# A chunked linear-attention block in fp32: correction products from two inverses, key work moved to GpSimd, keys kept unexpanded

## Chip, cores and metric

The kernel runs on one core of one Trainium2 chip. The metric is the device time of one execution in microseconds (us). Engines are named as in the profile: PE is TensorE (PEld its weight loads), DVE is VectorE, ACT is ScalarE, POOL is GpSimd, SP is SyncE.

## What is computed

Input is one sequence of 4096 tokens of width 256, all in fp32. A layer norm with modulation is followed by an attention without a softmax over tokens, and then by a mixture of experts. Cut to what matters:

```python
q, k, v = x @ Wq, x @ Wk, x @ Wv              # 8 heads of 64
beta, tg = sigmoid(x @ Wbeta), sigmoid(x @ Wtg)   # 8 modes a head
qr = l2norm(rotary(q, cos, sin)) * scale      # angles = pos * omega[h, m] * inv_freq
kr = l2norm(rotary(k, cos, sin))
g  = log(clip(tg * rho, 1e-6))
def step(S, inp):                             # one token; 64 memories (head, mode) of 64x64
    S  = S * exp(g_t)
    kv = k_t . S
    dv = (v_t - kv) * beta_t
    S  = S + k_t (x) dv
    o_t = q_t . S
x = x + ga * ((sum over modes of mode_w * o) * sigmoid(x @ Wg)) @ Wo
# then: layer norm, router, top 2 of 8 experts, capacity 1024, gelu, weighted sum
```

## The kernel before

**Tiles, halves, chunks.** The recurrence is worked in chunks of 32 tokens. A tile is 128 tokens (4 chunks), and there are 32 tiles. A tile is done in two halves (hh = 0 and 1), each of 4 heads; the 64 modes and heads are held as 16 groups ("quads") of 4 modes, 8 to a half. Partitions carry mode (4) x frequency or token (32). `u = 2n + hh` counts halves. The loop body of each engine is `half(n, 1)` followed by `half(n + 1, 0)`, so the jump back to the loop's start falls between an hh = 0 half and the hh = 1 half behind it.

**What a half does.** It prepares its own keys, queries and decays, builds the triangular systems of its 4 chunks, and inverts them on DVE (`solve`, L1226: 31 steps of two passes, then a transpose that writes `tt` and raises `tt_ready`, L1240). In the meantime the four chunks of the half before (called v) go through the chain of the memories, chunk after chunk:

- PE `memory_read` (L535): keys times state, into `bank_mem`; keys come from `ke`, which is expanded so that a key of 32 rows stands in a 128-row block with zeroes.
- DVE `right_sides` (L1242): times the decay `eg_col`, and the values minus that, into `rhs`.
- PE `corrections` (L553): the inverse `tt` times `rhs`, in 32x32 tiles of the array (L563), and then the state times the queries (L569).
- ACT `take_dv` (L760): fades the state (L765) and copies the corrections to `dv` (L769). DVE `decayed_corrections` (L1258) scales them to `dvs`.
- PE `update_and_outputs` (L573): expanded turned keys `kte` times `dvs` (L582), and the outputs (L590).
- DVE `update_memories` (L1266): adds the update to the state and takes the outputs.

Then the next chunk's `memory_read` may start.

**Where the keys come from.** PE replicates keys and queries (`replicate`, L485). DVE rotates keys (`rotate_keys`, L1175: four products and two sums), POOL rotates queries from ACT's copy `raw` (L1485 to L1490, `q_rotated`). ACT expands the rotated keys (`expand_ke`, L796, 4 passes a chunk) and the keys that DVE turned (`turn_keys`, L1202; `expand_kte`, L752, 4 passes a chunk). PE `gram` (L497) makes the products of keys with keys and queries for a chunk, and DVE `chunk_systems` (L1219) takes them. DVE also works out the six passes of `angle_parts` (L1112) for the next half; PE `turn_sums` (L624) uses them.

**What sets the order.** Every engine runs its own `half` in the order that is written there; a wait holds up all that is behind it. On PE (L644) the replications and the decay rows stand between the chunks of the chain, `gram(u, 0)` behind the corrections of chunk 3, and the other three behind its update. On ACT (L816) sine and cosine stand between chunks 0 and 1, the copies `raw` and the exponentials of the decays between chunks 1 and 2. On DVE (L1332) the chain's passes are woven between its own work.

## Time and profile before

| | |
|---|---|
| runs of the kernel before | 7991.04, 8003.09, 8010.95 us (median 8003.09) |
| the profiled execution | 7953.85 us, span 7951.7 us |
| mean granted TensorE clock | 0.82 of full speed |
| PE busy, x instructions | 5413.0 us (68%), 111401 |
| DVE busy, x instructions | 5656.2 us (71%), 11457 |
| ACT busy, x instructions | 3642.4 us (46%), 7127 |
| POOL busy, x instructions | 1241.2 us (16%), 740 |
| HBM traffic | 11 GB/s over the span |

Busy time is an average over three stages: a set-up of some 200 us, the loop over tiles up to about 7330 us, and the experts with their combination behind that. The change touches only the first two. One fp32 matmul of the source is two MATMUL instructions in the profile, each with its LDWEIGHTS. In the timeline a row is a run of like instructions on one engine: start, length, engine, line, operation, tiles and shapes, their count, and in brackets the idle time before it and what ended that.

### The profile page before, as it was taken

The page shows a single profiled execution, that of the slowest core. Times are in us where ns is not written, and L with a number is a line of the kernel's source. Part 1 is how long each engine was busy: PE and PEld are TensorE (multiplying, and loading weights), DVE is VectorE, ACT ScalarE, POOL GpSimd, SP SyncE. Part 2 cuts the span into 40 slices and gives each one's busy share as a digit, 9 for nine tenths or more (in the row PEclk, how much of TensorE's full clock was granted, in tenths as well). Part 3 has the DMA queues.
Part 4 walks back from the last instruction along what each step waited for, and adds up shares of the span by engine and source line. Part 5 has one row for each costly group of instructions (what it writes and reads, how often), then busy time and mean ns, then how long its engine had stood idle before and what let it go on. Part 6 is the DMA issues. An engine that isn't in the chain of part 4 may idle for free. (4 is left out here: it accounts for less than half of the span.)

```text
span 7951.7 us, 264166 instructions
## 1 busy us (share of the span) xinstructions
PE 5413.0 (68%) x111401; PEld 4716.2 (59%) x111401; DVE 5656.2 (71%) x11457; ACT 3642.4 (46%) x7127; POOL 1241.2 (16%) x740
## 2 busy tenths in 40 slices
PE   0676667666776677666766667666676667766994
PEld 0666656556666666566665666556666556655663
DVE  6777777777777777777777787777777777776003
ACT  0454445544544455544544455544454445554220
POOL 0111111111111111111111111111111111111003
PEclk9787888777877787887878888888887888887997
DMA  2000000000000000000000000000000000000223
GB/s 75 2 6 6 6 6 4 4 6 6 6 6 6 6 4 6 4 6 6 6 6 6 6 4 6 4 6 6 6 6 6 6 6 4 6 4 9 87 75 95
DMA packets 60431, 104.35 MB, mean 13 GB/s; under 512 B 11296, under 2 KB 48736, under 8 KB 58080
## 3 DMA queue, kind: packets, MB, share of 16 engines
q1 hardware_dynamic: 50784, 61.66, 2.4%
q0 software_dynamic: 8448, 25.18, 1.0%
q8 instruction: 940, 15.40, 0.8%
q14 instruction: 259, 2.12, 0.1%
HBM read 53.25 MB, written 33.55 MB: 11 GB/s over the span
## 5 line engine op out<-in xcount | busy, mean ns | idle before, releaser
L765 ACT ACTIVATE state<-state,gc_end 128x128 f32<-128x128 f32 x2048 | 650.1, 389 | 1432.4 <-PE bank L569 1430.9
L563 PE MATMUL bank<-rhs,tt 32*32 32x64 f32 x16384 | 407.0, 248 | 874.7 <-DVE rhs L1256 874.6
L563 PEld LDWEIGHTS bank<-rhs,tt 32*32 32x32 f32 x16384 | 316.3, 125 | 961.5 <-issue 944.4
L582 PE MATMUL last_two<-dvs,kte 128*64 128x64 f32 x16384 | 716.4, 254 | 150.3 <-DVE dvs L1263 150.3
L634 PE MATMUL bank<-tmp,turn_mat 32*32 32x128 f32 x24576 | 745.3, 279 | 48.4 <-issue 34.1
L545 PE MATMUL bank<-state,ke 128*64 128x64 f32 x16384 | 647.3, 246 | 167.3 <-issue 128.8
L582 PEld LDWEIGHTS last_two<-dvs,kte 128*64 128x64 f32 x16384 | 655.1, 167 | 164.9 <-DVE dvs L1263 157.2
L634 PEld LDWEIGHTS bank<-tmp,turn_mat 32*32 32x32 f32 x24576 | 709.8, 110 | 71.5 <-issue 65.4
L800 ACT ACTIVATE ke<-kq 32x512 f32<-32x512 f32 x1024 | 641.9, 627 | 238.1 <-DVE kq L1191 226.0
L545 PEld LDWEIGHTS bank<-state,ke 128*64 128x64 f32 x16384 | 605.2, 159 | 238.9 <-issue 184.2
L1239 DVE TENSOR_TENSOR last_two<-last_two,prod 128x31 f32<-128x31 f32 (+15 forms) x1984 | 692.5, 349 | 68.1
L506 PE MATMUL bank<-kq,ke 128*64 128x64 f32 x16384 | 638.6, 250 | 124.1 <-DVE pw L1224 115.6
L1237 DVE TENSOR_TENSOR prod<-bd,last_two 128x31 f32<-128x31 f32 (+15 forms) x1984 | 671.1, 338 | 68.3
L756 ACT ACTIVATE kte<-kt 32x512 f32<-32x512 f32 x1024 | 641.4, 626 | 142.9 <-PE last_two L582 125.0
L506 PEld LDWEIGHTS bank<-kq,ke 128*64 128x64 f32 x16384 | 617.8, 165 | 129.8 <-DVE pw L1224 77.6
L1272 DVE TENSOR_TENSOR state<-last_two,state 128x512 f32<-128x512 f32 x512 | 354.1, 692 | 205.1 <-PE last_two L582 172.9
L1263 DVE TENSOR_TENSOR dvs<-bank,dec_end 128x256 f32<-128x256 f32 x512 | 217.3, 424 | 363.3 <-PE bank L569 354.6
L1485 POOL TENSOR_TENSOR tmp<-raw,cos_t 128x1024 f32<-128x1024 f32 x64 | 151.2, 2362 | 2007.8 <-ACTq L839 2007.8
L480 PE MATMUL bank<-row_group,select 128*128 128x128 f32 x3072 | 434.4, 298 | 6.9 <-DVE tmp L1187 5.6
L569 PE MATMUL bank<-qg,state 128*64 128x32 f32 x8192 | 410.5, 250 | 0.3 <-issue 0.3
L480 PEld LDWEIGHTS bank<-row_group,select 128*128 128x128 f32 x3072 | 395.4, 207 | 24.7 <-DVE tmp L1187 6.4
L1461 POOL DMA_INDIRECT expert_rows<-xn,scatter_at x64 | 64.0, 999 | 2166.1 <-DVE scatter_at L1325 2156.3
(236 smaller groups left out, 9821.8 us busy)
## 6 DMA issues: line engine op xcount, KB each, us to landing
w_sb<-in_L_ffn_W_dram SPq DMA_DIRECT2D x16, 1024.0 KB, 9.6
expert_rows<-ke SPq DMA_DIRECT2D x1, 8192.0 KB, 21.0
xrows<-expert_rows SPq DMA_DIRECT2D x16, 512.0 KB, 8.7
expert_outputs<-yrow POOLq DMA_DIRECT2D x16, 512.0 KB, 3.4
xt<-_attn_hidden_states_dram SPq DMA_DIRECT2D x32, 128.0 KB, 2.4
xr<-_attn_hidden_states_dram SPq DMA_DIRECT2D x32, 128.0 KB, 3.0
x_after_attention<-xr SPq DMA_DIRECT2D x32, 128.0 KB, 1.7
xo<-x_after_attention SPq DMA_DIRECT2D x32, 128.0 KB, 3.6
```

What stands on the lines that cost most here:

```text
L480: mm = pe.matmul(b[:, ql * P:ql * P + P], select[:, b4 * 4 + ql, :], row_group[:, group, :], start=True, stop=True)
L506: mm = pe.matmul(b[s, q * 2 * C:(q + 1) * 2 * C], ke[:, c, r, q, s], kq[:, r, q, :, c * C:c * C + C], start=(r == 0), stop=(r == 1))
L545: mm = pe.matmul(bank_mem[g][s, q % 4 * DK:q % 4 * DK + DK], ke[:, c, r, q, s], state[:, hh * HQ + q, r, :], start=(r == 0), stop=(r == 1))
L563: pe.matmul(bank_mem[g][s, q % 4 * DK:q % 4 * DK + DK], tt[s, c, q, :], rhs[s, q, :], start=True, stop=True)
L569: mm = pe.matmul(out_bank(g, side), state[:, hh * HQ + q, r, :], qg[:, r, q, c * C:c * C + C], start=(j == 0 and r == 0), stop=False)
L582: mm = pe.matmul(bank_upd[g][s, (q % 4) * P + r * DK:(q % 4) * P + r * DK + DK], kte[:, r, q, s], dvs[:, q, :], start=True, stop=True)
L634: mm = pe.matmul(b[s, ql * P:ql * P + P], turn_mat[s, 2 * i + kind, hh * HQ + q, :], tmp[s, part, q * P:q * P + P], start=(i == 0), stop=( ...
L756: ins = act.activation(kte[s, :, :, 32 * m:32 * m + 32].rearrange("p r q f -> p (r q) f"), kt[s, :, :, c * C:c * C + C].rearrange("p r q f ...
L765: ins = act.activation(state[:, vh * HQ + q], state[:, vh * HQ + q], ACT.Copy, scale=gc_end[:, vh, q, c:c + 1])
L800: ins = act.activation(ke[s, c, :, :, 32 * m:32 * m + 32].rearrange("p r q j -> p (r q) j"), kq[s, :, :, 0, c * C:c * C + C].rearrange("p ...
L1237: ln(dve.tensor_tensor(pr, a_prob[:, j + 1:C, j:j + 1].broadcast_to([P, rows, cols]), t_prob[:, j:j + 1, 0:cols].broadcast_to([P, rows, co ...
L1239: ln(dve.tensor_tensor(below, below, pr, ALU.subtract))
```

## The change

The chain's corrections become two products a chunk: `tt` times the values, plus `tt_eg` (the inverse times the decay, made by POOL) times the negated read `ks`, which ACT copies. DVE's `right_sides` and `decayed_corrections` are gone. The update uses `dv` itself; the decay to the chunk's end is put on the turned keys by POOL (`fade_keys`, in place). The expanded `ke` and `kte` are gone: reads, updates and `gram` use 32x32 tiles over four modes where they used two sides of 64 columns. POOL adds the products of the key rotation, and takes over `angle_parts`. DVE's order changes with it.

```diff
 def gram(u, hh, c):
     pe.wait_ge(sem("q_rotated"), since("q_rotated", u + 1))
-    pe.wait_ge(sem("ke_ready"), 4 * u + c + 1)
+    pe.wait_ge(sem("k_rotated"), since("k_rotated", u + 1))
...
-                for s in SIDES:
-                    mm = pe.matmul(b[s, q * 2 * C:(q + 1) * 2 * C], ke[:, c, r, q, s],
-                                   kq[:, r, q, :, c * C:c * C + C], start=(r == 0), stop=(r == 1))
+                for s in MODES:
+                    mm = pe.matmul(b[s, q * 2 * C:(q + 1) * 2 * C], kq[s, hh, r, q, 0, c * C:c * C + C],
+                                   kq[s, hh, r, q, :, c * C:c * C + C], start=(r == 0), stop=(r == 1))
 def memory_read(v, hh, c):
...
-                for s in SIDES:
-                    mm = pe.matmul(bank_mem[g][s, ...], ke[:, c, r, q, s], state[:, hh * HQ + q, r, :], ...)
+                for s in MODES:
+                    mm = pe.matmul(bank_mem[g][s, ...], kq[s, hh, r, q, 0, c * C:c * C + C],
+                                   state[s, hh * HQ + q, r, :], ...)
 def corrections(v, hh, c):
-        pe.wait_ge(sem(f"rhs_ready{g}"), since(f"rhs_ready{g}", vc + 1))
+        pe.wait_ge(sem(f"ks_copied{g}"), since(f"ks_copied{g}", vc + 1))
+        pe.wait_ge(sem("v_ready"), v + 1)
         pe.wait_ge(sem("tt_ready"), v + 1)
+        pe.wait_ge(sem("tt_eg_ready"), vc + 1)
...
-                pe.matmul(bank_mem[g][s, ...], tt[s, c, q, :], rhs[s, q, :], start=True, stop=True)
+                pe.matmul(bank_mem[g][s, into], tt[s, c, q, :], v_sb[s, c, q // 2 * DK:...], start=True, stop=False)
+            for s in MODES:
+                pe.matmul(bank_mem[g][s, into], tt_eg[s, c, q, :], ks[s, q, :], start=False, stop=True)
 def update_and_outputs(v, hh, c):
-        pe.wait_ge(sem(f"dvs_ready{g}"), since(f"dvs_ready{g}", vc + 1))
-        pe.wait_ge(sem("kte_ready"), vc + 1)
+        pe.wait_ge(sem(f"dv_ready{g}"), since(f"dv_ready{g}", vc + 1))
+        pe.wait_ge(sem("kt_faded"), v + 1)
...
-                                   kte[:, r, q, s], dvs[:, q, :], start=True, stop=True)      # s in SIDES
+                                   kt[s, hh, r, q, c * C:c * C + C], dv[s, q, :], ...)        # s in MODES
 # ACT
-def expand_kte(v, c): ...
-def expand_ke(v, c): ...
-def take_dv(v, vh, c): ...
+def chain(v, vh, c):
+    for g in range(2):
+        act.wait_ge(sem(f"ks_full{g}"), since(f"ks_full{g}", vc + 1))
+        act.activation(ks[:, 4 * g:4 * g + 4, :]..., bank_mem[g][:, 0:4 * DK], ACT.Copy, scale=-1.0)  # ks_copied
+    for g in range(2):
+        act.wait_ge(sem(f"dv_full{g}"), vc + 1)
+        act.activation(dv[...], bank_mem[g][:, 0:4 * DK], ACT.Copy)      # dv_ready
+        for q in range(4 * g, 4 * g + 4):
+            act.activation(state[...], state[...], ACT.Copy, scale=gc_end[...])   # state_faded
 # DVE, half()
-    memories(right_sides, 0); memories(decayed_corrections, 0)      (and for chunks 1 to 3)
+    unit_length(u)
     memories(update_memories, 0)
-    unit_length(u)
...
+    decays(u, hh, 0, first)
+    decays(u, hh, 1, first)
     memories(update_memories, 1)
+    rotate_keys(u)            # the four products; POOL adds them up
     memories(update_memories, 2)
     beta_decays(u, hh)
-    turn_keys(u, first)
+    turn_keys(u, hh)          # waits for POOL's k_rotated
     chunk_systems(u, 0)
     queries_for_memories(u, hh)
     memories(update_memories, 3)
-    angle_parts(n2, hh2, ...)  (two passes in front of each of chunk_systems 1 to 3)
 # POOL
 def half(n, hh, first=False, last=False):
     pool.wait_ge(sem("replicated"), u + 1)
     pool.wait_ge(sem("cos_ready"), u + 1)
     ln(pool.tensor_tensor(r4, q1, co, ALU.mult))
     ln(pool.tensor_tensor(r5, q2, si, ALU.mult))
     ln(pool.tensor_tensor(kq[:, hh, 0, :, 1, :], tm[4], tm[5], ALU.add))
+    pool.wait_ge(sem("k_products"), 2 * u + 1)
+    ln(pool.tensor_tensor(kq[:, hh, 0, :, 0, :], tm[0], tm[1], ALU.add))
+    pool.wait_ge(sem("k_products"), 2 * u + 2)
+    vec(pool.tensor_tensor(kq[:, hh, 1, :, 0, :], tm[3], tm[2], ALU.subtract), "k_rotated", u + 1)
     ln(pool.tensor_tensor(r4, q2, co, ALU.mult))
     ln(pool.tensor_tensor(r5, q1, si, ALU.mult))
     vec(pool.tensor_tensor(kq[:, hh, 1, :, 1, :], tm[4], tm[5], ALU.subtract), "q_rotated", u + 1)
+    if not last:
+        angle_parts(*after(n, hh))       # the same six passes, on POOL
+    fade_keys(u, hh)                     # kt *= dec at the chunk's end, 2 passes of 128x1024; kt_faded
     if not last and hh == 1:
         group_rows(n + 1)
+    inverse_for_reads(u, hh, first)      # waits for tt_ready; tt_eg = tt * eg_col, 4 passes of 128x256
     if hh == 0 and not first:
         scatter(n - 1)
```

`kt` and `kq` become double (one for each half), `tmp` grows from 4 to 6 slices, and `pos` is advanced by POOL. Values, gates, roots, `solve`, the routing and the experts are as before.

## Rows read from the trace of the kernel before

**Rows 1.** The page, busy time of the engines over the whole span.
```profile
PE 5413.0 (68%) x111401; PEld 4716.2 (59%) x111401; DVE 5656.2 (71%) x11457; ACT 3642.4 (46%) x7127; POOL 1241.2 (16%) x740
```

**Rows 2.** One line's instructions: the copy that stands once a tile, first and last start.
```profile
L1154 DVE COPY col<-bank x32: 291/291/292, 218.5 to 7103.7; 128x128 f32<-128x128 f32 x32
```

**Rows 3.** Groups by line, 200 to 7300 us: busy us, mean ns of one, idle before.
```profile
L1256 DVE TENSOR_TENSOR rhs<-v_sb,rhs 128x256 f32<-128x256 f32 x506 | 316.7, 626 | 68.2 <-issue 51.8
L1263 DVE TENSOR_TENSOR dvs<-bank,dec_end 128x256 f32<-128x256 f32 x505 | 214.4, 424 | 357.7 <-PE bank L569 349.1
...
L1117 DVE TENSOR_TENSOR tmp<-pos,omega 128x1024 f32<-128x1024 f32 x63 | 77.2, 1226 | 9.0 <-DVE outT L1274 4.7
```

**Rows 4.** Timeline of DVE: end of an hh = 0 half, the loop's jump.
```profile
4102.65 1.89 DVE L1240 STREAM_TRANSPOSE tt<-last_two 128x1024 f32<-128x1024 f32 x1
...
4109.21 0.16 DVE L1330 TENSOR_TENSOR gate_w<-rt 128x2 f32 x1
4112.56 0.42 DVE L1253 TENSOR_TENSOR rhs<-bank,eg_col 128x256 f32<-128x256 f32 x1 [3.19 <-issue]
4114.71 0.43 DVE L1256 TENSOR_TENSOR rhs<-v_sb,rhs 128x256 f32<-128x256 f32 x1 [1.73 <-issue]
```

**Rows 5.** Timeline of PE in the hh = 1 half behind it: four marks.
```profile
4115.38 1.07 PE L563 MATMUL bank<-rhs,tt 32*32 32x64 f32 x32 [12.90 <-DVE rhs L1256]
...
4126.27 0.65 PE L563 MATMUL bank<-rhs,tt 32*32 32x64 f32 x32
...
4157.86 3.61 PE L506 MATMUL bank<-kq,ke 128*64 128x64 f32 x64
...
4174.12 3.72 PE L517 MATMUL bank<-wv_sb,hT 128*128 128x256 f32 x16
```

**Rows 6.** Timeline: end of that hh = 1 half and start of the next.
```profile
4218.23 1.89 DVE L1240 STREAM_TRANSPOSE tt<-last_two 128x1024 f32<-128x1024 f32 x1
...
4221.30 1.07 PE L563 MATMUL bank<-rhs,tt 32*32 32x64 f32 x32 [7.39 <-DVE rhs L1256]
...
4233.50 0.65 PE L563 MATMUL bank<-rhs,tt 32*32 32x64 f32 x32
```

**Rows 7.** Windows: us, busy PE, PEld, DVE, ACT, POOL, granted clock, DMA share, GB/s.
```profile
4126.00:4142.00 16.00, 13.89 (x348) 10.01 (x346) 10.67 (x18) 11.69 (x21) 1.99 (x1) 1.00 0.01 3
...
4210.00:4221.00 11.00, 3.90 (x66) 3.65 (x65) 9.99 (x27) 0.00 (x0) 0.57 (x2) 0.50 0.00 0
```

**Rows 8.** Timeline of PE at the full clock: runs of its small matmuls.
```profile
4012.28 0.65 PE L563 MATMUL bank<-rhs,tt 32*32 32x64 f32 x32
...
4013.45 0.65 PE L563 MATMUL bank<-rhs,tt 32*32 32x64 f32 x32
...
4014.52 1.13 PE L582 MATMUL last_two<-dvs,kte 128*64 128x64 f32 x32
...
4052.92 3.93 PE L506 MATMUL bank<-kq,ke 128*64 128x64 f32 x128
...
4068.31 5.44 PE L634 MATMUL bank<-tmp,turn_mat 32*32 32x128 f32 x192
```

**Rows 9.** One line's instructions, 4000 to 4060 us: shortest, median, longest ns of one.
```profile
L563 PE MATMUL bank<-rhs,tt x256: 211/215/312, 4000.3 to 4043.7; 32*32 32x64 f32 x128
```

**Rows 10.** Timeline of ACT and POOL between chunks 1 and 2 of the chain.
```profile
4139.29 0.60 ACT L838 ACTIVATE raw<-bank 128x512 f32<-128x512 f32 x1 [0.26 <-PE bank L489]
...
4140.01 2.36 POOL L1485 TENSOR_TENSOR tmp<-raw,cos_t 128x1024 f32<-128x1024 f32 x1 [28.39 <-ACTq L839]
...
4142.48 1.26 ACT L765 ACTIVATE state<-state,gc_end 128x128 f32<-128x128 f32 x4
```

**Rows 11.** Groups by line on POOL, 200 to 7300 us, columns as in rows 3.
```profile
L1486 POOL TENSOR_TENSOR tmp<-raw,sin_t 128x1024 f32<-128x1024 f32 x64 | 207.1, 3236 | 5.0
...
L1485 POOL TENSOR_TENSOR tmp<-raw,cos_t 128x1024 f32<-128x1024 f32 x64 | 151.2, 2362 | 2007.8 <-ACTq L839 2007.8
```

**Rows 12.** Timeline of POOL in the set-up: copies with one input.
```profile
159.60 4.31 POOL L1434 COPY select<-cmat 32x1024 f32<-32x1024 f32 x4
```

More of the change, by code:

```diff
@@ L794, in roots @@
                     act.activation(ew[0:64, :], gb[0:64, :], ACT.Exp).then_inc(sem("eg_raw"), 1)
-            def expand_ke(v, c):
-                for m in range(4):
-                    s = slice(32 * m, 32 * m + 32)
-                    ins = act.activation(ke[s, c, :, :, 32 * m:32 * m + 32].rearrange("p r q j -> p (r q) j"),
-                                         kq[s, :, :, 0, c * C:c * C + C].rearrange("p r q j -> p (r q) j"), ACT.Copy)
-                ins.then_inc(sem("ke_ready"), 1)
-            def next_expansions(v, c):
-                act.wait_ge(sem("upd_full1"), since("upd_full1", 4 * v + c))
-                expand_kte(v, c)
             def clear_inverse(v, first):
@@ L820, in half @@
                 if not first:
-                    take_dv(v, vh, 0)
-                    act.wait_ge(sem("upd_full1"), since("upd_full1", 4 * v + 1))
-                    expand_kte(v, 1)
+                    chain(v, vh, 0)
                 act.wait_ge(sem("turns_ready"), u + 1)
@@ L830, in half @@
                 if not first:
-                    take_dv(v, vh, 1)
-                    act.wait_ge(sem("k_rotated"), since("k_rotated", u))
+                    chain(v, vh, 1)
                     act.wait_ge(sem("q_rotated"), since("q_rotated", u))
                 for s in range(2):
-                    if s == 0 and not first:
-                        act.wait_ge(sem("upd_full1"), since("upd_full1", 4 * v + 2))
-                        expand_kte(v, 2)
                     take(lambda b: act.activation(raw[:, s].rearrange("p h t -> p (h t)"), b[:, :], ACT.Copy))
@@ L844, in half @@
                 if not first:
-                    take_dv(v, vh, 2)
-                act.wait_ge(sem("k_rotated"), since("k_rotated", u + 1))
-                expand_ke(u, 0)
+                    chain(v, vh, 2)
                 if not first:
-                    act.wait_ge(sem("upd_full1"), since("upd_full1", 4 * v + 3))
-                    expand_kte(v, 3)
-                expand_ke(u, 1)
-                if not first:
-                    take_dv(v, vh, 3)
-                expand_ke(u, 2)
-                expand_ke(u, 3)
+                    chain(v, vh, 3)
                 clear_inverse(v, first)
@@ L859, in half @@
                     act.activation(stat2[:, 8:9], stat2[:, 7:8], ACT.Sqrt, bias=eps_ln[:]).then_inc(sem("std2_ready"), 1)
-                if not first:
-                    act.wait_ge(sem("rhs_ready1"), since("rhs_ready1", 4 * v + 4))
                 for c2 in range(2):
@@ L881, in half @@
                     gap(n - 1)
-                if not first:
-                    act.wait_ge(sem("upd_full1"), since("upd_full1", 4 * v + 4))
-                act.wait_ge(sem("kt_ready"), u + 1)
-                expand_kte(u, 0)
             def route(t):
@@ L907, in _ @@
             for c in range(NC):
[L908 to L910 removed]
+                chain(v, 1, c)
             act.wait_ge(sem("var2_ready"), NT)
@@ L1154, in take_columns, with decays @@
                 free(dve.tensor_copy(col[:].rearrange("p c a q -> p (c a q)"), b[:, 0:NC * 2 * Q]))
-            def decays(u, hh, b4):
+            def decays(u, hh, b4, first):
                 b = full()
+                if b4 == 0 and not first:
+                    dve.wait_ge(sem("kt_faded"), u)
                 s4 = slice(4 * b4, 4 * b4 + 4)
@@ L1400, in _ @@
             weigh_decays(0)
-            angle_parts(0, 0, range(6))
             turns_mod_1(0, 0)
```

254 lines of the change are left out of this document (107 added, 147 removed).

## The prediction

> **What bounds the kernel now.** I read the page first: no engine is full, DVE is nearest with 71% [rows 1]. The copy that stands once a tile gives the pace, (7103.7 - 218.5) / 31 = 222.1 us a tile, 111 a half [rows 2]. The chain's groups on DVE show that much of its idle time is spent on PE: 357.7 us before the `dvs` passes alone [rows 3]. So the half is two stretches. In one the four chunks of memories run as a chain over PE, ACT and DVE; in the other DVE inverts the systems alone. The timelines show the joints. After an hh = 0 half, `tt` is ready at 4102.65 + 1.89 = 4104.54, the routing ends at 4109.37, the jump back costs DVE 3.19 us and another 1.73 [rows 4], and the first corrections start only at 4115.38 [rows 5]. After an hh = 1 half it takes 4221.30 - 4220.12 = 1.2 us [rows 6]. I use the start of chunk 1's corrections as my zero ("C1": 4126.27 and 4233.50 in rows 5 and 6), since the first chunk runs at half clock (1.2 of 2.4 GHz; granted 0.50 before it, 1.00 after C1 [rows 7]; the same 32 instructions take 1.07 and 0.65 us [rows 5]).
>
> **DVE's relief is no term of the sum.** It loses per half 8 products of 0.42 [rows 4], 8 differences of 0.63 and 8 `dvs` passes of 0.42 [rows 3], the two sums of the keys and six angle passes of up to 1.23 [rows 3]: 3.4 + 5.0 + 3.4 + 2.5 + about 6 = 20 us. But it then waits for the chain; I follow the chain.
>
> **PE's price.** Reads, updates and `gram` issue twice the matmuls, in 32x32 tiles. A run of 32 such takes 0.65 us, of which one's own 0.215 [rows 8, 9]: (0.65 - 0.215) / 31 = 14 ns apart. The 64-column form stands (1.13 - 0.22) / 31 = 29 ns apart, with 0.22 as my estimate of one's length from rows 9. So two for one cost nothing (28 against 29), if the pace holds in long runs. The corrections add 32 x 14 = 0.45 us a group to 1.17 (4013.45 - 4012.28 [rows 8]): 1.62, or 3.25 a chunk; at half clock 0.9 a group. The update now changes tile shape around the outputs; I give it 1.4 us a group, against about 1.2, for the change, which no row prices alone. A read is 128 x 14 = 1.8.
>
> **Joint after hh = 0.** POOL's first scaled inverse, 128x256, is bounded by a quarter of a full pass, 0.6 us, and a full one, 2.4 [rows 11]; 0.8 is likeliest, since its data is a quarter. PE starts 0.9 us after `tt` and has its first update about 8.5 after it. DVE isn't there: routing and jump put its first instruction at +8.0 (4112.56), and if the second gap stays, its first addition at +10.2 (4114.71) [rows 4]. Two additions with outputs (1.9), the last read group (1.0) and the decay rows (2.0) give C1 at +15.2. Before, it was 4126.27 - 4104.54 = 21.7 [rows 4, 5]. Gain 6.5, bounds 3 (PE slower, DVE's jump longer) and 8.
>
> **Joint after hh = 1.** No routing or jump. The start comes 0.3 earlier, but two groups at half clock cost 1.8 more, of which some 0.5 comes back as the clock rises before the update. Loss 1.0, bounds 0 and 2.5.
>
> **From C1 to the fourth `gram`'s end**, before: 4174.12 - 4126.27 = 47.85 us [rows 5] (47.9 in the other half as well). After, from zero: corrections to 3.3, updates to 6.1, replication for DVE to 8.0, read of chunk 2 to 9.9, replication for ACT to 11.8, ACT's second `raw` to 12.4. ACT then does its table load and three exponentials, which took 4142.48 - 4139.89 = 2.6 us [rows 10], and only behind them copies `ks` for chunk 2: its corrections start at 15.4, with PE idle for 3.6. Updates to 21.5, decay rows 23.5, read 25.3, corrections of chunk 3 to 28.6. Here POOL is late: it starts at 12.5 and needs eight passes for `q_rotated` where it needed six. Two of the six took 3.24 and not 2.36 [rows 11]; they coincide with DVE's sums of the keys, which go. I take 8 x 2.44 = 19.5, so `gram` 0 starts at 32.0 (before: 4157.86 - 4126.27 = 31.6). The bounds are 8 x 2.4 and 8 x 3.3. The Trainium skill, GPSIMD Engine Reference, section Specifications, says the interface is contended while DVE reads two SBUF inputs. By that rule the new passes run free, since DVE's products read PSUM; the trace's 2.36 beside 3.24 agrees. Half clock for that `gram`, as now (3.61 [rows 5]): 35.5. The last two decay-row groups with the first system 2.0, the last update 2.9, three `gram`s 5.4, switches 0.3: 46.1. Gain 1.8 a half, bounds a gain of 3.5 (full clock) and a loss of 5 (POOL at 3.2 a pass).
>
> **What is hidden.** The angle passes end about 12 to 15 us after `q_rotated` (three of 2.4, three between one-input copies of 1.1 [rows 12] and 2.4), and their readers stand behind values and gates; `fade_keys` adds 5, ready a solve ahead of its use. Neither costs anything; if POOL took 10 us more, `turn_sums` would stall DVE's solve. ACT loses its 32 expansion passes a half and gains 8 copies, but nothing waited for the expansions alone, so nothing is gained there. The hh = 1 tail (values, mode weights, root) is a chain of its own and keeps its length. DVE's added wait on `kt_faded` stands long after that event. The first angle parts, now on POOL with nothing beside them, cost 5 us once.
>
> **Sum.** 6.5 - 1.0 + 2 x 1.8 = 9.1 us a tile; over 31.5 tiles 287, less 5: 282 us off the profiled execution's 7953.85, so 7672. That execution is 0.6% under the median of the runs, 8003; on the median it is 7721, so **7720 us**.
>
> **Rivals.**
> *Issue pace (slower).* Tiles 14 ns apart are only shown in runs of 32, which may have been queued up before their start; the one long run of 32x32 tiles, 192 of 128 columns, has (5.44 - 0.27) / 191 = 27 ns [rows 8], though streaming may set that. If 27 is a floor, about 1,800 instructions on the path of a half cost 13 ns more, 23 us, less POOL's slack of 3.4: 20 us a half, 64 halves, 1,250 us, so some 8,950. It decides from (4.5 + 3.4) / 1,800 = 4.4 ns over 14, that is from about 18.5 ns; at 20 ns it gives about 8,100. For it: the other forms of rows 8 stand at 27 to 29 ns. Against: both of the short runs start behind other matmuls and keep 14 ns to their end. The Trainium skill, TensorEngine Tiling, section Instruction Overhead, has some 60 cycles for each matmul, 25 ns at 2.4 GHz. By that rule the doubled matmuls would cost nearly the floor's price; the row with 14 ns speaks against it for short runs, and no row shows a long one. Chance 0.2.
> *POOL slow (slower).* If its passes stay at 3.2 with the transposes of DVE beside them, `gram` 0 comes 6 us later in each half: +390 us, about 8,100. For it: two of six passes do so now. Chance 0.1.
> *Gain eaten.* The clock falls after the two new idle stretches of PE (3.6 and 3.4 us), and chunk 2 and the last update run at half clock, 3 to 4 us a half: 7,900 to 8,020. For it: a granted 0.50 wherever PE idles long [rows 7]. Chance 0.15.
> *Chain freer than I have it.* Full clock through all `gram`s and a jump without the second gap: 14 us a tile, 7,550. Chance 0.1.
> *My forecast*, 7,620 to 7,850: 0.45.
> That the change does not do what it says has no chance here, since the passes vanish from the code.
>
> **How the numbers follow.** A measurement can tell about 0.3%, 24 us. Faster by more: 0.45 + 0.1 + two thirds of 0.15, 0.65; within: 0.05; slower: 0.2 + 0.1 = 0.30. The range leaves out the floor's far end and a little at the fast one: 7560 to 8280.
>
> **What would show it.** DVE busy falls by some 1,200 us, while its idle before the state additions rises. ACT's `ks` copy of chunk 2 starts just behind the exponentials, with PE idle 3 to 4 us before. `gram` 0's idle is ended by POOL's `q_rotated`. PE's runs of 64 and 128 small tiles stand 14 ns apart. C1 comes some 15 us after `tt` at both joints. I am wrong if those runs stand over 18 ns apart, if POOL's passes stay near 3.2 us, or if `turn_sums` waits for the angle parts.

## The result and the profile after

The changed kernel takes **8340.22 us** (median of 4 runs, 8328.57 to 8376.47) against 8006.41 us for the kernel before on the same chip: ratio **1.0429**, 95% interval 1.0399 to 1.0458. The prediction said 7720 us, in a range that ended at 8280. The profiled execution has a span of 8374.8 us.

The page after, of its first and third part:

```profile
span 8374.8 us, 392787 instructions
...
PE 5930.7 (71%) x176937; PEld 5073.8 (61%) x176937; DVE 4235.2 (51%) x9313; ACT 2562.7 (31%) x5591; POOL 2926.3 (35%) x1667
...
q8 instruction: 1470, 24.08, 1.2%
```

Against [rows 1], DVE has lost 1,421 us of work and ACT 1,080. Neither loss shows in the time. PE has 176,937 matmuls where it had 111,401. The last line is the queue that brings instructions: 24.08 MB in 1470 packets, 16.4 KB each. By the counts, 392,787 instructions in 1470 packets, one packet holds some 260 instructions, or, on PE, 128 matmuls with their 128 weight loads.

PE's waits after, from the view of waits: who waited for what, us in total, times, longest.

```profile
PE bank L566 <- POOL tt_eg L1418: 363.6, 64, 24.2
PE bank L505 <- issue: 356.2, 268, 2.1
PE bank L566 <- ACT ks L764: 235.5, 63, 3.8
...
PE bank L545 <- issue: 177.3, 104, 3.4
...
PE last_two L588 <- issue: 97.2, 131, 1.6
```

`tt_eg` is the wait at the joints, where PE waits in any case, and `ks` is chunk 2's wait for ACT, as forecast: 235.5 / 63 = 3.7 us. The other three are new or have grown: before, the read (L545) had 128.8 us of such waits in 60 times, and `gram` and the update had none. "Issue" means that nothing the profile shows held the engine, and it stands before the `gram` (L505), the read (L545) and the update (L588), the three products that went over to 32x32 tiles. The timeline of PE shows it best, here the end of an hh = 1 half that answers to the last two marks of [rows 5]:

```profile
4102.49 0.75 PE L505 MATMUL bank<-kq 32*32 32x64 f32 x36
4104.18 1.53 PE L505 MATMUL bank<-kq 32*32 32x64 f32 x92 [0.94 <-issue]
...
4111.54 1.99 PE L505 MATMUL bank<-kq 32*32 32x64 f32 x128 [0.82 <-issue]
4115.57 2.50 PE L505 MATMUL bank<-kq 32*32 32x64 f32 x127 [2.05 <-issue]
4119.34 4.22 PE L505 MATMUL bank<-kq 32*32 32x64 f32 x129 [1.26 <-issue]
4123.49 1.86 PE L516 MATMUL bank<-wv_sb,hT 128*128 128x256 f32 x7
```

Read the start times and the counts together. The last three runs start at 4111.54, 4115.57 and 4119.34, 4.0 and 3.8 us apart, and each is 128 matmuls long, give or take one. Within the first of them, at the full clock, the matmuls stand (1.99 - 0.22) / 127 = 14 ns apart, as forecast (the last, at a granted 0.53, takes 4.22 us); then PE stands still for 1 to 2 us, with nothing in the profile to wait for. 128 matmuls is one packet of instructions. The DMA view of 4108 to 4124 agrees, with four packets in 16 us, 3.2 to 4.4 us apart (each number is for 0.4 us):

```profile
GB/s 0 0 0 41 0 0 0 0 0 0 0 41 0 0 0 0 0 0 0 0 0 41 0 0 0 0 0 0 0 0 0 0 41 0 0 0 0 0 0 0
```

So I take as theory **S**: PE gets a packet of 256 instructions every 4 us or so; what it has in stock runs at 14 ns a tile, and a long stretch of small tiles runs the stock empty. Its rivals are **F**, no such limit, the tiles cost nothing and the loss is elsewhere; and **C**, the loss is chunk 2's wait for ACT and the half clock behind it.

Where the time is, by the prediction's own stretches (C1 is the start of chunk 1's corrections), in us:

| stretch | before | forecast | after |
|---|---|---|---|
| `tt` to C1, after hh = 0 | 21.7 | 15.2 | 4066.45 - 4050.62 = 15.8 |
| C1 to the fourth `gram`'s end, hh = 1 half | 47.85 | 46.1 | 4123.49 - 4066.45 = 57.0 |
| `tt` to C1, after hh = 1 | 13.4 | 14.4 | 4183.13 - 4169.58 = 13.6 |
| C1 to the fourth `gram`'s end, hh = 0 half | 47.9 | 46.1 | 4241.30 - 4183.13 = 58.2 |

The marks of the last column that the timeline above lacks:

```profile
4048.72 1.90 DVE L1186 STREAM_TRANSPOSE tt<-last_two 128x1024 f32<-128x1024 f32 x1
4066.45 0.31 PE L566 MATMUL bank<-v_sb,tt 32*32 32x64 f32 x8
...
4167.69 1.89 DVE L1186 STREAM_TRANSPOSE tt<-last_two 128x1024 f32<-128x1024 f32 x1
4183.13 0.31 PE L566 MATMUL bank<-v_sb,tt 32*32 32x64 f32 x8
...
4241.30 2.89 PE L605 MATMUL bank<-wo_sb,outT 128*128 128x256 f32 x8
```

A tile takes (7471.0 - 206.6) / 31 = 234.3 us after, by the copy that gave 222.1 before [rows 2]. In this tile the joints came near the forecast. The two long stretches cost 57.0 + 58.2 - 92.2 = 23.0 us a tile more than forecast, and that is the whole of the error, 234.3 - 213.0 = 21.3 (the rest of the tile gave 1.7 back). One tile is not quite the mean: over all tiles of the loop the medians of the four stretches, in the order of the table, are 22.2, 49.3, 13.2 and 48.7 before, and 17.0, 56.6, 14.5 and 57.0 after. By them the joint after hh = 0 also takes 1.8 us more than forecast.

### The profile page after: what moved, and what is told of

It reads as the page before. It is cut to its first block and busy times, and to the rows that moved or that the text cites. A ratio compares the mean times of both kernels' runs of the same rounds, so it can differ in the third digit from the quotient of the medians.

```text
span 8374.8 us, 392787 instructions
## 1 busy us (share of the span) xinstructions
PE 5930.7 (71%) x176937; PEld 5073.8 (61%) x176937; DVE 4235.2 (51%) x9313; ACT 2562.7 (31%) x5591; POOL 2926.3 (35%) x1667
## 3 DMA queue, kind: packets, MB, share of 16 engines
q8 instruction: 1470, 24.08, 1.2%
## 5 line engine op out<-in xcount | busy, mean ns | idle before, releaser
L566 PE MATMUL bank<-v_sb,tt 32*32 32x64 f32 x16384 | 679.2, 255 | 640.0 <-POOL tt_eg L1418 363.6
L566 PEld LDWEIGHTS bank<-v_sb,tt 32*32 32x32 f32 x16384 | 474.8, 129 | 734.4 <-issue 709.8
L505 PE MATMUL bank<-kq 32*32 32x64 f32 x32768 | 614.4, 228 | 374.8 <-issue 356.2
L505 PEld LDWEIGHTS bank<-kq 32*32 32x32 f32 x32768 | 546.9, 113 | 427.6 <-issue 421.7
L588 PE MATMUL last_two<-dv,kt 32*32 32x64 f32 x32768 | 723.1, 242 | 98.0 <-issue 97.2
L545 PE MATMUL bank<-state,kq 32*32 32x64 f32 x32768 | 659.6, 242 | 180.0 <-issue 177.3
L545 PEld LDWEIGHTS bank<-state,kq 32*32 32x32 f32 x32768 | 597.5, 124 | 269.5 <-issue 255.0
L640 PE MATMUL bank<-tmp,turn_mat 32*32 32x128 f32 x24576 | 733.8, 276 | 21.9 <-DVE lg L1218 12.4
L568 PE MATMUL bank<-ks,tt_eg 32*32 32x64 f32 x16384 | 679.0, 254 | 35.3 <-issue 35.3
L588 PEld LDWEIGHTS last_two<-dv,kt 32*32 32x32 f32 x32768 | 607.4, 123 | 151.9 <-issue 121.6
L568 PEld LDWEIGHTS bank<-ks,tt_eg 32*32 32x32 f32 x16384 | 507.6, 133 | 40.4 <-issue 40.0
```

The lines of the kernel that those rows point to most:

```text
L505: mm = pe.matmul(b[s, q * 2 * C:(q + 1) * 2 * C], kq[s, hh, r, q, 0, c * C:c * C + C], kq[s, hh, r, q, :, c * C:c * C + C], start=(r == 0) ...
L545: mm = pe.matmul(bank_mem[g][s, q % 4 * DK:q % 4 * DK + DK], kq[s, hh, r, q, 0, c * C:c * C + C], state[s, hh * HQ + q, r, :], start=(r == ...
L566: pe.matmul(bank_mem[g][s, into], tt[s, c, q, :], v_sb[s, c, q // 2 * DK:q // 2 * DK + DK], start=True, stop=False)
L568: pe.matmul(bank_mem[g][s, into], tt_eg[s, c, q, :], ks[s, q, :], start=False, stop=True)
L588: mm = pe.matmul(bank_upd[g][s, (q % 4) * P + r * DK:(q % 4) * P + r * DK + DK], kt[s, hh, r, q, c * C:c * C + C], dv[s, q, :], start=True ...
L640: mm = pe.matmul(b[s, ql * P:ql * P + P], turn_mat[s, 2 * i + kind, hh * HQ + q, :], tmp[s, part, q * P:q * P + P], start=(i == 0), stop=( ...
```

## The experiments

Ratios are to the kernel before on the same chip, with 95% intervals. Experiments 1 to 4 share a chip, 5 to 8 another, 9 and 10 a third, and 11 has a fourth.

**1. The pace of each form by itself.** In the set-up of the kernel before, where PE stands idle for long, four runs of matmuls on weights that are loaded anyway, into banks not yet in use. They are tiles of 128 columns, tiles of 64, the 128x64 form of before with 64, and tiles of 16 (the profile counts each of these f32 products as two matmuls with a weight load each):

```diff
             pe.wait_ge(sem("mod_used"), 1)
+            quarters = [slice(32 * m, 32 * m + 32) for m in range(4)]
+            sides = [slice(0, 64), slice(64, 128)]
+            for i in range(48):
+                for s in quarters:
+                    pe.matmul(banks[4][s, 0:128], wv_sb[s, 0, 0:32], wg_sb[s, 0, 0:128], start=True, stop=True)
+            for i in range(96):
+                for s in quarters:
+                    pe.matmul(banks[5][s, 0:64], wv_sb[s, 0, 0:32], wg_sb[s, 0, 0:64], start=True, stop=True)
+            for i in range(96):
+                for s in sides:
+                    pe.matmul(banks[6][s, 0:64], wv_sb[:, 0, 0:64], wg_sb[:, 0, 0:64], start=True, stop=True)
+            for i in range(96):
+                for s in quarters:
+                    pe.matmul(banks[7][s, 0:16], wv_sb[s, 0, 0:32], wg_sb[s, 0, 0:16], start=True, stop=True)
```

> The kernel before, with four long runs of matmuls put into PE's idle time in the set-up: 384 instructions in 32x32 tiles with 128 columns, 768 in tiles with 64 columns, 384 of the 64-column form on two sides with 64 columns, 768 in tiles with 16 columns. Theory S (PE is supplied with instructions at about 256, that is 128 matmuls with their weight loads, in 4 us, and faster only out of a stock): the 64-column tiles start 14 ns apart and fall to about 31 ns a matmul in the long run, with gaps of 1 to 2 us put down to issue, and the tiles with 16 columns also stand at about 31. Rival F (no supply limit; streaming sets the pace): 27, 14, 29 and under 10 ns, with no gaps. The whole time is within 0.3% of before in both.

The timeline of PE in that run's set-up:

```profile
39.46 13.51 PE L421 MATMUL bank<-wg_sb,wv_sb 32*32 32x128 f32 x384 [2.65 <-DVE gate_row L979]
52.80 0.94 PE L424 MATMUL bank<-wg_sb,wv_sb 32*32 32x64 f32 x50
53.90 1.99 PE L424 MATMUL bank<-wg_sb,wv_sb 32*32 32x64 f32 x128 [0.16 <-issue]
57.36 1.99 PE L424 MATMUL bank<-wg_sb,wv_sb 32*32 32x64 f32 x128 [1.47 <-issue]
61.37 2.77 PE L424 MATMUL bank<-wg_sb,wv_sb 32*32 32x64 f32 x128 [2.02 <-issue]
65.38 3.63 PE L424 MATMUL bank<-wg_sb,wv_sb 32*32 32x64 f32 x128 [1.24 <-issue]
69.39 1.99 PE L424 MATMUL bank<-wg_sb,wv_sb 32*32 32x64 f32 x128 [0.38 <-issue]
...
77.14 10.57 PE L427 MATMUL last_two<-wg_sb,wv_sb 128*64 128x64 f32 x334 [0.77 <-issue]
...
92.64 1.68 PE L430 MATMUL last_two<-wg_sb,wv_sb 32*32 32x16 f32 x128 [2.20 <-issue]
96.10 1.91 PE L430 MATMUL last_two<-wg_sb,wv_sb 32*32 32x16 f32 x128 [1.79 <-issue]
```

The 64-column tiles come in runs of 128 that start 4.0 us apart (57.36, 61.37, 65.38, 69.39), 31 ns a matmul over the whole; whether a run itself takes 1.99 us at the full clock or 3.63 at a granted 0.50 changes nothing in when the next one starts. Tiles of 16 columns, a quarter of the work, still start 3.5 us apart, 27 ns a matmul where S expected 31. So the columns don't set the difference between 3.5 and 4.0: the first 64-column interval (53.90 to 57.36) is 3.5 as well. The tiles of 128 columns can't tell the theories apart: behind a slow start they go at 6.00 / 228 = 26 ns (46 to 52 us), without a pause, and so draw a packet in 3.4 us. The 128x64 form takes (10.57 - 0.22) / 333 = 31 ns a matmul: long runs of it go at the same pace as the small tiles, and each of its matmuls does the work of two. Its weight loads show that it meets the same limit, though only just:

```profile
77.14 3.81 PEld L427 LDWEIGHTS last_two<-wg_sb,wv_sb 128*64 128x64 f32 x128 [0.90 <-issue]
81.15 3.81 PEld L427 LDWEIGHTS last_two<-wg_sb,wv_sb 128*64 128x64 f32 x128 [0.20 <-issue]
85.16 2.41 PEld L427 LDWEIGHTS last_two<-wg_sb,wv_sb 128*64 128x64 f32 x78 [0.20 <-issue]
```

They too come in runs of 128 that start 4.0 us apart, 29 ns apart within a run, with a pause of 0.20 us. The pace is one of instructions, not of work, and it stands in a kernel with no dependency around it; the whole kernel took 7952.47 us against 7934.68, within the 0.3% that both theories allowed. Theory S holds and F falls. What sets the 3.5 to 4.0 us a packet is left open: no run here looked further than that.

The Trainium skill, Runtime: NRT & Kernel Launch, section Instruction fetch mechanics, says that instructions come in blocks of 16 KiB, 256 of them, and that crossing a block's edge is "mostly hidden". The size agrees with the 16.4 KB a packet; for the small tiles the trace disagrees on the cost, 0.2 to 2.2 us of idle PE between the runs above.

**2. The `gram` alone in tiles, in the kernel before.**

```diff
+                    pe.sem_inc(sem("pe_held"), 1)
...
-                            for s in SIDES:
-                                mm = pe.matmul(b[s, q * 2 * C:(q + 1) * 2 * C], ke[:, c, r, q, s],
-                                               kq[:, r, q, :, c * C:c * C + C], start=(r == 0), stop=(r == 1))
+                            for s in MODES:
+                                mm = pe.matmul(b[s, q * 2 * C:(q + 1) * 2 * C], kq[s, r, q, 0, c * C:c * C + C],
+                                               kq[s, r, q, :, c * C:c * C + C], start=(r == 0), stop=(r == 1))
```

> The kernel before with one part of the change alone: the gram products in 32x32 tiles from the unexpanded keys, 128 matmul instructions a chunk where there were 64; ACT still expands the keys for the reads. Theory S: a gram takes up to 4 us in place of 2, three of them in a row behind the last update; 3 to 6 us a half, 200 to 400 us slower (8200 to 8400). Rival F: tiles at 14 ns against 29 cost nothing; within 0.5% of before.

8040.21 us, 1.0128 (1.0085 to 1.0171): 105 us slower, below S's band and above F's nothing. Its waits show the new entry:

```profile
PE bank L564 <- DVE rhs L1257: 868.4, 190, 24.1
...
PE bank L507 <- issue: 169.5, 128, 2.1
```

It is small here for a reason that the same view gives: before, a `gram` waited once a half, 115.6 us in all, for DVE's `pw`, and now 25.3. So 90 of the 169.5 us of issue replace idle time that was there, and 79 are new. The kernel also still stops for `rhs` 190 times; that the stock fills up meanwhile is what S says, not something this run shows by itself. The sign is S's, the size is not.

**3. The `gram` alone back in the wide form, in the changed kernel.**

```diff
-                            for s in MODES:
-                                mm = pe.matmul(b[s, q * 2 * C:(q + 1) * 2 * C], kq[s, hh, r, q, 0, c * C:c * C + C],
-                                               kq[s, hh, r, q, :, c * C:c * C + C], start=(r == 0), stop=(r == 1))
+                            for s in SIDES:
+                                mm = pe.matmul(b[s, q * 2 * C:(q + 1) * 2 * C], kq[:, hh, r, q, 0, min(c * C, 2 * C):min(c * C, 2 * C) + 2 * C],
+                                               kq[:, hh, r, q, :, c * C:c * C + C], start=(r == 0), stop=(r == 1))
```

> The changed kernel with the gram products in the old 64-column form over all 128 rows, half the matmul instructions, and the same streaming time. It leaves out the separation of the modes in these products (each sums over several modes), so only its time counts. Theory S: the gaps put down to issue between the grams go, and the four grams with what stands between them fall by 4 to 7 us a half, 250 to 450 us faster than the changed kernel (7890 to 8090). Rival F with the loss elsewhere (half clock in chunk 2, waits for banks or for POOL): no change, 8300 to 8380.

7900.74 us, 0.9966 (0.9941 to 0.9991), 4.6 points below the change's 1.0429 (taken on another chip; on a third it was 1.0397, experiment 8). The stretch from C1 to the fourth `gram`'s end fell from 57.0 to 4099.49 - 4049.21 = 50.3 us in the hh = 1 half. Theory C has nothing to say to this, as chunk 2's wait is still there.

**4. Chunk 2's copy ahead of the raw copies, in the changed kernel.** `copy_reads` is the part of `chain` that copies `ks`.

```diff
                     act.wait_ge(sem("q_rotated"), since("q_rotated", u))
+                if not first:
+                    copy_reads(v, 2)
                 for s in range(2):
...
-                    chain(v, vh, 2)
+                    chain(v, vh, 2, copied=True)
```

> The changed kernel with ACT's copy of the reads of chunk 2 put ahead of its copies of the replicated queries, so that chunk 2's corrections don't wait for the exponentials of the decays. Theory C (the loss is the wait of PE for that copy and the half clock behind it): PE's 3.7 us of idle time and the half-clock corrections go, 4 to 7 us a half, 250 to 450 us faster than the changed kernel. Theory S: the chunk comes forward by 3 to 6 us, but PE's supply and POOL's turned queries, due 33 us after chunk 1's corrections, bound the rest: 0 to 150 us faster (8190 to 8340).

8244.19 us, 1.0388 (1.0345 to 1.0431). The wait for `ks` is gone, chunk 2 starts 12.8 us after C1 (4035.26 - 4022.43) where it started 17.2 after it. Yet the stretch only fell to 4076.11 - 4022.43 = 53.7, and the ratio by 0.4 points, or 0.1 against experiment 8, within the intervals. PE's waits in this run:

```profile
PE bank L505 <- issue: 275.8, 198, 2.1
PE bank L545 <- issue: 199.4, 118, 3.4
PE bank L505 <- POOL kq L1441: 186.9, 64, 14.1
PE last_two L588 <- issue: 127.5, 158, 1.8
```

The 235.5 us of waits for `ks` are gone, and the first `gram` now waits 186.9 us for POOL's rotated queries, of which 14.1 were there: 173 of the 235 come back in the next wait. The waits for issue have grown at reads and updates (177.3 to 199.4, 97.2 to 127.5) and fallen at the `gram` (356.2 to 275.8). Theory C, which wanted 250 us or more, falls; the better evidence is that experiments 3 and 5 keep chunk 2's wait and yet take most or all of the loss away.

**5 to 8, on one chip.** In the changed kernel the `gram`, the reads and the updates in the wide form (5); experiments 3 and 4 together (6); a change of order in the kernel before (7); and the changed kernel itself (8). Number 5 is this on top of number 3:

```diff
-                            for s in MODES:
-                                mm = pe.matmul(bank_mem[g][s, q % 4 * DK:q % 4 * DK + DK], kq[s, hh, r, q, 0, c * C:c * C + C],
-                                               state[s, hh * HQ + q, r, :], start=(r == 0), stop=(r == 1))
+                            for s in SIDES:
+                                mm = pe.matmul(bank_mem[g][s, q % 4 * DK:q % 4 * DK + DK], kq[:, hh, r, q, 0, min(c * C, 2 * C):min(c * C, 2 * C) + 2 * C],
+                                               state[:, hh * HQ + q, r, :], start=(r == 0), stop=(r == 1))
...
-                            for s in MODES:
...
-                                               kt[s, hh, r, q, c * C:c * C + C], dv[s, q, :], start=True, stop=True)
+                            for s in SIDES:
...
+                                               kt[:, hh, r, q, min(c * C, 2 * C):min(c * C, 2 * C) + 2 * C], dv[:, q, :], start=True, stop=True)
```

> The changed kernel with the gram, the memory reads and the state updates all in the 128x64 form (32 rows of a mode are no longer kept apart: the products sum over the modes of a 64-row side and over neighbouring chunks' columns, so the values differ; shapes, waits and all other engines' work stay). PE records fall from 160,553 (gram alone in that form) to about 127,800. Theory S (PE is given about 256 instructions, 128 weight loads and 128 matmuls, per 4 us, and small tiles run out of them): less than the 0.9966 of the kernel before that the gram alone gave, 0.965 to 0.985, as 256 fewer records a half relieve the stretch from the corrections of chunk 1 to the fourth gram. Theory F (no limit of supply, the gram's form mattered by itself): within 0.3% of 0.9966, as reads and updates take the array 14 ns a tile against 29 ns in the wide form. Theory C (chunk 2's wait for ScalarE and the half clock behind it are the loss): no change either, since the wait stays.

7522.58 us, **0.943** (0.9392 to 0.9468), further than any theory had it. In the hh = 1 half the stretch from C1 is 4116.69 - 4070.68 = 46.0 us, against 46.1 in the prediction. Its marks in that half:

```profile
4085.90 0.35 PE L566 MATMUL bank<-v_sb,tt 32*32 32x64 f32 x8 [3.74 <-ACT ks L764]
4102.67 3.35 PE L505 MATMUL bank<-kq 128*64 128x64 f32 x64 [1.75 <-POOL kq L1434]
4110.55 3.93 PE L505 MATMUL bank<-kq 128*64 128x64 f32 x128
4114.67 2.08 PE L505 MATMUL bank<-kq 128*64 128x64 f32 x64 [0.19 <-DVE pw L1170]
```

Chunk 2 waits 3.74 us for ACT (forecast 3.6), the first `gram` starts at +32.0 behind POOL (forecast 32.0) and at half clock (forecast so). This is the schedule that I had worked out: it is right for a PE that never runs out of instructions. Over all tiles the medians of the four stretches are 15.0, 46.0, 13.0 and 44.8 us, so the wide form also takes 2.0 and 1.5 us off the joints. The waits for issue at the `gram` and nearly all at the update are gone.

Number 6, the edits of 3 and 4 in one kernel:

> The changed kernel with the gram in the 128x64 form (values differ, as above) and with ScalarE's negated copy of chunk 2's read ahead of the raw copies. Either edit alone: 0.9966 and 1.0388 of the kernel before (the change itself 1.0429). Theory S: while instructions were short, the 3.7 us wait of chunk 2 only let the stock refill, so taking it away gained 0.4%; with the gram relieved it is worth more, 0.970 to 0.988. Theory C: the same 0.4% whatever the gram's form would refute it again; it wants 0.965 or less. If GpSimd's rotation of the queries, which ends about 34 us after the corrections of chunk 1, then holds the first gram: 0.990 to 0.997.

7861.05 us, 0.9855 (0.9816 to 0.9895), inside S's band: 1.1 points for the copy's place on top of the 0.9966, where it gave 0.4 while PE was short. The intervals of these differences, taken on two chips, are as wide as the difference, so this alone would not settle anything. Here too the wait for `ks` gave way to one for POOL's rotated queries, 203.2 us in 64 times.

Number 7, in VectorE's `half` of the kernel before (`slots_ranks` is the first half of `slots`, cut off behind the reductions):

```diff
-                memories(right_sides, 0)
-                memories(decayed_corrections, 0)
...
                 solve(u, hh, meanwhile)
+                right_sides(u, hh, 0)
+                if hh == 0 and not first:
+                    slots_ranks(n - 1)
+                decayed_corrections(u, hh, 0)
                 if hh == 0 and not first:
                     slots(n - 1)
```

> The kernel before, with VectorE's right sides and decayed corrections of chunk 0 moved to the end of the half that ends with tt, the first before and the second between the two parts of the router's slot arithmetic (22 small operations, 4.7 us, that stand between tt and the right sides in the joint after hh=0). Nothing is removed. Theory O (the 6.5 us that the change gained in that joint came from the order, since the corrections no longer stand behind the slots and the stall of 3.2 us at the loop's edge, not from VectorE's lighter load): about 5 us a tile, 0.979 of before, 0.970 to 0.988. Rival: the joint's gain is given back in the stretch behind it, where TensorE's instructions or GpSimd's rotation of the queries are late: 0.995 to 1.003.

7805.25 us, **0.9788** (0.9749 to 0.9827). From `tt` to C1 after hh = 0 it takes 4018.78 - 4000.68 = 18.1 us, against 21.7 in [rows 4, 5]. So 3.6 us of the 5.9 that the change gained in that joint are to be had by order alone, with no work taken off DVE. The timeline of DVE shows the corrections of chunk 0 done before the loop's jump (3.33 us of issue), which used to stand ahead of them:

```profile
4000.80 0.43 DVE L1253 TENSOR_TENSOR rhs<-bank,eg_col 128x256 f32<-128x256 f32 x1
...
4006.13 0.43 DVE L1263 TENSOR_TENSOR dvs<-bank,dec_end 128x256 f32<-128x256 f32 x1 [0.69 <-PE bank L569]
...
4008.94 0.16 DVE L1333 TENSOR_TENSOR gate_w<-rt 128x2 f32 x1
4012.43 0.69 DVE L1272 TENSOR_TENSOR state<-last_two,state 128x512 f32<-128x512 f32 x1 [3.33 <-issue]
```

The whole gain is 178 us or 5.6 a tile. By the medians over all tiles 4.0 of it is in this joint (18.2 for 22.2) and 1.2 in the stretch behind it (48.1 for 49.3).

Number 8, the changed kernel:

> The changed kernel itself, on the chip of the three runs beside it, so that they can be compared with it directly. 1.035 to 1.050 of the kernel before; a ratio outside would say that the size of the loss depends on the chip.

8298.08 us, 1.0397 (1.0354 to 1.0441), as expected. On this chip the wide form of all three products takes 8298.08 - 7522.58 = **775 us** off the change, in a kernel that leaves out the separation of the modes.

**9 and 10. The change's corrections with the wide products of before.** Nothing is left out of this kernel and of the two behind it. It is the kernel before with these parts of the change:

```diff
-        dvs = sb("dvs", [P, HQ, DK])
-        dec_end = sb("dec_end", [P, 2, HQ, NC])
+        tt_eg = sb("tt_eg", [P, 2, HQ, C])
...
+                            pe.matmul(bank_mem[g][s, into], tt[s, c, q, :], v_sb[s, c, q // 2 * DK:q // 2 * DK + DK], start=True, stop=False)
...
+                            pe.matmul(bank_mem[g][s, into], tt_eg[s, c % 2, q, :], ks[s, q, :], start=False, stop=True)
...
-                                               kte[:, r, q, s], dvs[:, q, :], start=True, stop=True)
+                                               kte[:, r, q, s], dv[:, q, :], start=True, stop=True)
...
-                    take_dv(v, vh, 0)
+                    chain(v, vh, 0)
...
+                fade_keys(u)
...
+                inverse_for_reads(u, hh, first, (0, 1))
```

`gram`, reads, updates and the expansions of keys on ACT are those of before, `right_sides` and `decayed_corrections` are gone, and chunk 2's copy stands where experiment 4 put it. ACT's chain of chunk 3 stands ahead of `expand_ke(u, 1)`, and DVE's order follows the change's. `tt_eg` is a ring of two chunks, half its size in the change.

> The change's corrections without its small tiles elsewhere: the kernel before (keys expanded by ScalarE, gram, reads and updates in the 128x64 form, key rotation and angle parts on VectorE) with the corrections as two inverse products a chunk (ScalarE's negated copy of the read, GpSimd's inverse scaled for the reads in a ring of two chunks, GpSimd's faded keys ahead of ScalarE's expansion) and chunk 2's copy ahead of the raw copies. About 127,800 PE records, as in the run with all products in the wide form. Theory S (the change's loss is TensorE's supply of instructions): the corrections' own idea pays once the other small tiles are gone, 0.940 to 0.970 of before (the wide-form run gave 0.943 with a lighter VectorE and ScalarE). Rival A (ScalarE, which now has the expansions and the copies in one line, becomes the bound of the stretch behind the corrections of chunk 1): 0.980 to 1.010. Rival D (the gain of the wide-form run came from VectorE's and GpSimd's shifted work, not from TensorE): 1.00 or more.

7715.04 us, **0.9729** (0.9698 to 0.9759), a little above S's band, which ended at 0.970, and below both rivals'. The corrections' idea pays as soon as it comes without the tiles. Experiment 7 gained 2.1% by order alone, so one may ask whether this is the same gain. It isn't in the main: by the medians over all tiles the two long stretches fell from 49.3 and 48.7 us to 44.3 and 44.6, where experiment 7 had 48.1 and 48.9. How the rest divides between the new corrections and DVE's new order, no run here tells.

Experiment 10 adds the change's `angle_parts` on GpSimd, in place of VectorE's, behind `q_rotated`.

> The same with the angle parts moved from VectorE to GpSimd, as in the change (six passes a half, 18 us there). The prediction counted this relief of VectorE as no term: within 0.4% of the run beside it. If VectorE's passes between the chunk systems and the substitution set the end of a half (1.23 and 0.7 us each, about 5 us a half on VectorE): 2 to 4% less than the run beside it. If GpSimd's passes come late for the turn sums: 1% or more above it.

7590.34 us, **0.9575** (0.9544 to 0.9607), 125 us, 1.6% or 2.0 us a half less than the run beside it: clearly more than the 0.4% of the prediction's reading, a little under the band of the other. PE's waits say where it came from, first of 9, then of 10:

```profile
PE bank L469 <- DVE sin_t L1149: 386.9, 31, 12.5
...
PE bank L505 <- DVE pw L1238: 111.2, 63, 2.4
```

```profile
PE bank L469 <- DVE sin_t L1131: 341.9, 31, 12.4
PE bank L565 <- ACT ks L769: 285.5, 129, 3.2
...
PE bank L638 <- POOL tmp L1449: 61.3, 31, 2.1
```

In 9 the last `gram` waits 1.8 us (111.2 / 63) for a bank that DVE frees only behind two angle passes; in 10 that wait is not among PE's ten largest, and a smaller one for POOL's parts has taken its place once a tile. The wait for DVE's `sin_t`, once a tile, has fallen by 45 us.

**11. Chunk 1's copy ahead of the sines.** The second fence just above has 129 waits for `ks`, two a half. One of them, 3.2 us, is chunk 1's:

```profile
3989.84 0.44 PE L565 MATMUL bank<-v_sb,tt 32*32 32x64 f32 x8 [3.20 <-ACT ks L769]
```

```diff
                     expand_kte(v, 1)
+                    copy_reads(v, 1)
...
-                    chain(v, vh, 1)
+                    chain(v, vh, 1, copied=True)
```

> The hybrid with the angle parts on GpSimd, and with ScalarE's copy of chunk 1's read ahead of the cosines and sines of the half (it stood behind them: TensorE waited 3.2 us for it in each half, at the chunk-1 corrections). If the wait goes and nothing takes its place: 3 us a half, 190 us, 0.933 of before (0.930 to 0.942). Rival: the queries' rotation on GpSimd, which starts behind the sines and the raw copies, then holds the first gram, and 1 to 3 us of it come back: 0.945 to 0.957.

7280.52 us, **0.917** (0.9149 to 0.9192), the fastest kernel of this study, against 1.0429 for the change. Against experiment 10, scaled by the kernel before on each chip, that is 4.05 points or some 320 us, 5.0 a half, for a wait of 3.2, and more than the band of either theory. The timeline of PE in the hh = 1 half has C1 and the end:

```profile
4121.12 0.31 PE L565 MATMUL bank<-v_sb,tt 32*32 32x64 f32 x8
...
4162.47 3.72 PE L516 MATMUL bank<-wv_sb,hT 128*128 128x256 f32 x16
```

The first matmuls of chunk 1 take 0.31 us where they took 0.44 behind the wait, and the granted clock stays at 1.00 from 4120 to 4160:

```profile
4120.00:4160.00 40.00, 36.67 (x1081) 31.96 (x1081) 24.73 (x37) 34.72 (x71) 25.07 (x12) 1.00 0.01 4
```

In 10 the 16 products of the outputs at the start of chunk 1 take 1.07 us behind the 3.2 us of idle, at a granted 0.50 (3989.84 to 3994); here they take 0.66 us. From C1 to chunk 2's corrections it takes 4004.13 - 3989.84 = 14.3 us in 10 and 4133.54 - 4121.12 = 12.4 in 11. So the wait cost its own length, 3.2, and 1.9 of slow clock after it: the 5.0.

## Why the prediction was wrong

**The step that failed** is in PE's price: "So two for one cost nothing (28 against 29), if the pace holds in long runs." It doesn't hold. 14 ns is the pace of what PE has in stock; over more than a packet the small tiles go at 31 ns a matmul (experiment 1), the same as the wide form, which does twice the work in each. Where the prediction priced a `gram` at 1.8 us, the three in a row take 4.0, 3.8 and 4.2. The joints, where PE waits, carried most of the doubling (2.0 and 1.5 us are lost there, by experiment 5); the stretches behind them didn't. With the wide form back the stretch takes 46.0 us for a forecast of 46.1, and its marks agree, so no other term in it was far off.

**The row that should have warned** was there, in [rows 8]: `x128` in 3.93 us for the wide form. I read it as what that form takes, 29 to 31 ns; it is also one packet of instructions in 4 us. Experiment 1 shows that the two nearly coincide: 3.81 us for the loads of a run and 0.20 of pause. The kernel before stood at the edge of the limit, and the page's count of instructions, set against the packets of its queue, would have given the size of a packet. From one row it couldn't be known which of the two set the 3.93.

**The rival that named it**, *Issue pace*, had the side, and 0.2. Its mechanism was off: it was put as a floor on each matmul, which prices short and long runs alike and gave 8,950 (7,720 and its 1,250 make 8,970). A supply with a stock costs only what a stretch draws beyond it, hence 8,340. What I held against it, that "both of the short runs start behind other matmuls and keep 14 ns to their end", was no evidence: a run of 32 is a quarter of a packet. Nor was the sign that I had set, runs over 18 ns apart: within a packet they keep 14, and the loss stands between the packets. The Trainium skill's some 60 cycles a matmul (TensorEngine Tiling, section Instruction Overhead), as an estimate 25 ns at 2.4 GHz, isn't the distance that the runs show between tiles either: 14 ns from stock and 31 without. Whether it holds for the matmuls of one tile, no run here tells.

**Joints.** Near: 15.8 for 15.2 and 13.6 for 14.4 in the tile shown, 17.0 and 14.5 as medians over all. The excess of 1.8 in the first is again PE's supply, as experiment 5 has 15.0 there. And the 6.5 us were not all the change's merit; experiment 7 has 3.6 of them by order.

**POOL's passes.** Right: all eight took 2.35 us (4080.65 to 4100.19), none 3.2. *POOL slow* falls. The angle passes with one input, though, were under-priced: "between one-input copies of 1.1 [rows 12] and 2.4" against these groups after:

```profile
L1394 POOL TENSOR_SCALAR tmp<-tmp 128x1024 f32<-128x1024 f32 x64 | 233.2, 3644 | 12.2 <-POOL tmp L1392 12.2
...
L1392 POOL TENSOR_SCALAR tmp<-tmp,cmat 128x1024 f32<-128x1024 f32 x64 | 182.3, 2849 | 13.5 <-POOL tmp L1390 13.5
...
L1395 POOL TENSOR_TENSOR tmp<-tmp 128x1024 f32<-128x1024 f32 x64 | 150.6, 2354 | 5.3
```

The six passes ended 18.3 us after `q_rotated`, not 12 to 15. That was hidden here, since the turn sums stand 27 us behind `q_rotated`.

**"DVE's relief is no term of the sum."** This contradicts the sum. Before, a `gram` waited for DVE's `pw` once a half, 63 times and 115.6 us in all. In the half of [rows 5] it is the last one:

```profile
4172.11 2.08 PE L506 MATMUL bank<-kq,ke 128*64 128x64 f32 x64 [2.28 <-DVE pw L1224]
```

The forecast let the three `gram`s follow each other in 5.4 us, and so took this wait away without naming it. The chunk systems, which free the banks of the `gram`, are DVE work on the path. In the change the waits for issue, 356.2 us before the `gram`, stand where this wait stood; in the hybrid, with PE supplied, the angle parts alone are worth 2.0 us a half (experiment 10).

**Chunk 2 behind the exponentials.** Right in size (3.7 for 3.6), and of no use as an explanation: it was in the sum, and taken away alone it gives 0.4% at most, since 173 of its 235 us come back as a wait for POOL's rotated queries (experiment 4). Whether it also gave the instructions time to arrive isn't shown.

## What to carry to other kernels

Count instructions as well as work: set the instruction queue's packets against the matmuls of the densest stretch, and where a stretch draws more than one packet per 4 us, try a form with fewer and larger matmuls, even if each small one takes half as long. Here it was worth 775 us. A pace read from a short run is that of a stock; before multiplying the number of instructions, look for a run longer than a packet, or make one in idle time. And when a wait of PE is removed, look at what stood behind it: the next wait may take its place (experiment 4, worth far less than its length), or it may have been lowering the clock (experiment 11, worth more).

## What was not expected of the hardware

- PE's long runs start one packet of 128 matmuls apart, 3.5 to 4.0 us, whatever is in them: 64 columns, 16 columns, or the 128x64 form.
- GpSimd's passes with one tensor input and scalars (2.85 to 3.64 us for 128x1024) are slower than those with two tensor inputs in the same series (2.35).
- One wait of 3.2 us a half cost about 5: the granted clock behind it was 0.50.
